# The last phase's final sum as an identity product on TensorE, and five of the eight groups of its norm on VectorE

## The reference

```python
x = x + _L1_conv_ref(_ln_c(x), ...)      # gate: (1x1 conv of y) * x3, added to x
t = _to_tokens(x)                        # points as rows, 96 channels
t = t + _L1_ffn_ref(_ln_t(t), L1_ffn_W1, L1_ffn_b1, L1_ffn_W2, L1_ffn_b2)
# _ln_t:  (v - mean) / sqrt(var + 1e-5) over the 96 channels
# _L1_ffn_ref: q_acc(relu(q_acc(q_mul(x) @ W1) + b1)) @ W2 + b2, q_mul = 8-bit floats, q_acc = 16-bit floats
x = _from_tokens(t, x)
```

## Time and profile before

| what | value |
|---|---|
| median of 3 runs | 3906.69 us (3899.2 to 3909.8) |
| profiled execution, its own time | 3896.73 us |
| its span, first to last instruction | 3894.9 us |
| busy over the span | PE 3001.9 us (77%), DVE 3198.1 us (82%), ACT 2883.9 us (74%), POOL 1723.6 us (44%) |
| phase C, from its first transfer's issue | 2730.99 us to the end |
| mean granted TensorE clock | 0.906 of full speed |

### The profile page before, as it was taken

The page is one execution under the profiler, slowest core; times in us unless marked ns, Lnnn a source line. Parts: engine busy times, 40 slices in busy tenths (PEclk is TensorE's granted clock), DMA queues, the critical chain, the costliest instruction groups (busy, mean ns, idle before and its releaser), DMA issues. The chain is left out here.

```text
span 3894.9 us, 67854 instructions
## 1 busy us (share of the span) xinstructions
PE 3001.9 (77%) x21476; PEld 1980.4 (51%) x21476; DVE 3198.1 (82%) x8112; ACT 2883.9 (74%) x6562; POOL 1723.6 (44%) x2404
## 2 busy tenths in 40 slices
PE   6777776777777777777767999998687878778786
PEld 5556565565655656565543444444344444444443
DVE  4888888888888888888875878888689888898987
ACT  2577777777777777777775555555599999999998
POOL 3777777777777777777650000000121222212121
PEclk8798888888888888888878999999799999999999
DMA  2232333323323232332126777776866666666662
GB/s 58 58 83 66 82 89 76 83 66 82 81 76 90 66 82 69 86 85 73 50 66 163 194 196 196 199 196 177 212 176 177 184 187 181 177 177 189 187 176 68
DMA packets 721626, 484.61 MB, mean 124 GB/s; under 512 B 420796, under 2 KB 700668, under 8 KB 708988
## 3 DMA queue, kind: packets, MB, share of 16 engines
q1 hardware_dynamic: 721276, 480.28, 46.8%
HBM read 278.37 MB, written 201.33 MB: 123 GB/s over the span
## 5 line engine op out<-in xcount | busy, mean ns | idle before, releaser
L1777 POOL TENSOR_SCALAR C_var<-C_st 128x16 f32<-128x16 f32 x64 | 16.6, 259 | 1538.3 <-DVE C_st L175 1538.3
L1404 DVE SCALAR_TENSOR_TENSOR B_y<-B_mid,B_coef,B_y 128x512 f32<-128x512 f32 x768 | 521.3, 747 | 139.5 <-ACT B_y L1371 139.5
L1324 PE MATMUL B_ps_row<-B_z,B_g 128*128 128x512 f32 x1152 | 520.0, 601 | 0.0
L375 DVE TENSOR_SCALAR A_hq<-A_h,A_b 128x512 f16<-128x512 f16 x768 | 294.4, 419 | 234.8 <-ACT A_h L367 228.7
L367 ACT ACTIVATE A_h<-A_hid 128x512 f16<-128x512 f32 x768 | 427.1, 591 | 64.2 <-PE A_hid L354 61.3
L175 DVE BATCH_NORM_STATS2 A_st<-A_xT 128x6 f32<-128x192 f32 x1536 | 443.9, 349 | 27.6 <-ACT A_xT L831 13.6
L367 ACT ACTIVATE C_h<-C_hid 128x512 f16<-128x512 f32 x768 | 426.1, 592 | 15.6 <-PE C_hid L354 8.1
L1444 ACT ACTIVATE C_q<-C_xT,C_shift,C_rstd 128x96 fp8e5<-128x96 f32 x1024 | 391.4, 456 | 45.8 <-POOL C_shift L1784 45.8
L861 ACT ACTIVATE A_xc<-A_xT,A_shift,A_rstd 128x96 f32<-128x96 f32 x1024 | 379.1, 456 | 0.0
L164 POOL TENSOR_TENSOR A_rstd<-A_var,A_expo 128x16 f32<-128x16 f32 x128 | 374.3, 2924 | 10.7
L668 PEld LDWEIGHTS A_fbank<-A_big_w,A_xq 97*128 97x128 f32 x2048 | 322.1, 228 | 29.8 <-issue 11.2
(11 more groups left out here) (160 smaller groups left out, 7314.0 us busy)
## 6 DMA issues: line engine op xcount, KB each, us to landing
A_xq<-in_x SPq DMA_DIRECT2D x32, 1536.0 KB, 8.9
x_scratch<-A_xT SPq DMA_DIRECT2D x64, 768.0 KB, 3.2
x_scratch<-A_x3h SPq DMA_DIRECT2D x64, 768.0 KB, 5.4
B_z<-x_scratch SPq DMA_DIRECT2D x96, 512.0 KB, 5.3
y_scratch<-B_y SPq DMA_DIRECT2D x96, 512.0 KB, 3.6
C_x3q<-x_scratch SPq DMA_DIRECT2D x32, 1536.0 KB, 9.1
C_y3q<-y_scratch SPq DMA_DIRECT2D x32, 1536.0 KB, 15.5
C_xT<-x_scratch SPq DMA_DIRECT2D x64, 768.0 KB, 15.7
```

What stands on the lines that cost most here:

```text
L375: r = dve.tensor_scalar(self.hq[:, b, s], self.h16[:, b, s], self.w["b1"][:, j:j + 1], 0.0, ALU.add, ALU.max)
L1324: m = pe.matmul(bank(c, h), g[c.buf(2)][:, d, :], z[c.buf(NB)][:, half(h), d:d + W], start=(d == 0), stop=(d == 2))
L1404: dve.scalar_tensor_tensor(y, mid[c.buf(2)][:, half(h), t:t + W], coef[c.buf(NB)][:, 3 + t:4 + t], y, ALU.mult, ALU.add).then_inc(ev["sums ...
```

## The change

The final sum of group k (residual plus y16b) is made by PE in PSUM: `result` multiplies y16b (16-bit) by a 96 x 96 identity into the bank and adds the four residual tiles as products with the 128 x 128 identity (before, four transposes into a bank of their own, and the sum on DVE). ACT evicts the bank to `outq` (`out` moves from DVE's list to ACT's). PE makes the sum of group s-2 in slot s behind pe_y (before, the transposes of group s-1 ahead of pe_y), that of group 7 in slot 0 of the next step, so that `steps` gets one step more; ACT evicts group s-3 in slot s, behind the hidden evictions. `dve_y` gets a wait for the sum two groups back. Of the norm's groups, 0, 3 and 6 stay on ACT; 1, 2, 4, 5 and 7 go to DVE as two instructions over the group's four tiles (times the scale, plus the shift), at the end of the slot that `LN_AT` gives; `LN_AT` is unchanged. POOL's waits for the norm follow.

```diff
+ACT_NORMS, DVE_NORMS = (0, 3, 6), (1, 2, 4, 5, 7)
 LN_AT = {6: (1, 0), 7: (1, 1), 8: (1, 2), 0: (0, 3), 2: (0, 4), 3: (0, 5), 4: (0, 6), 5: (0, 7)}
...
+    def norms_done(self, eng, i, k):
+        if k in ACT_NORMS:
+            eng.wait_ge(self.ev["norm2_act"], self.ev.at("norm2_act", i, ACT_NORMS.index(k)))
+        else:
+            eng.wait_ge(self.ev["norm2_dve"], self.ev.at("norm2_dve", i, DVE_NORMS.index(k)))
...
+    def dve_norm(self, dve, i, k):
+        ev, n = self.ev, DVE_NORMS.index(k)
+        t = slice(k * TPC, (k + 1) * TPC)
+
+        dve.wait_ge(ev["ln2"], ev.at("ln2", i, k // 4))
+        if n or begun(i - 1):
+
+            dve.wait_ge(ev["norm2_dve"], ev.at("norm2_dve", i, n) - 1)
+        dve.tensor_tensor(self.xs[:], self.x_of(i)[:, k * CW:(k + 1) * CW].rearrange("p (t c) -> p t c", c=C),
+                          per_token(self.rstd[:, t], TPC), ALU.mult).then_inc(ev["scaled2"], 1)
+        dve.wait_ge(ev["scaled2"], ev.at("scaled2", i, n))
+        dve.tensor_tensor(self.q8[:, t, :], self.xs[:], per_token(self.shift[:, t], TPC), ALU.add,
+                          saturate=False).then_inc(ev["norm2_dve"], 1)
...
-        pe.wait_ge(ev["norm2"], ev.at("norm2", i, k))
+        self.norms_done(pe, i, k)
...
         dve.wait_ge(ev["y16"], ev.at("y16", i, k))
+        if k >= 2:
+
+            dve.wait_ge(ev["c_full"], ev.at("c_full", i, k - 2))
+        elif begun(i - 1):
+            dve.wait_ge(ev["c_full"], ev.at("c_full", i - 1, NK - 2 + k))
...
-                back_uses += [("c", s - 1, 0, "out", s - 1), ("y", s - 1, 0, "y16", s - 1)]
...
+                back_uses.append(("y", s - 1, 0, "y16", s - 1))
+            if s >= 2:
+                back_uses.append(("c", s - 2, 0, "out", s - 2))
+            if s == 0:
+                back_uses.append(("c", NK - 1, -1, "out", NK - 1))
...
-            for n in range(-1, NQ):
+            for n in range(-1, NQ + 1):
...
-            def c_turn(i, k):
+            def result(i, k):
 
                 pe.wait_ge(ev["x1"], ev.at("x1", i, k))
-                bank_free(back, i, "c", k)
+                pe.wait_ge(ev["yb"], ev.at("yb", i, k))
+                bank_free(back, i if k < NK - 1 else i + 1, "c", k)
+                bank = back.bank("c", k)
+                pe.matmul(bank[0:C, 0:CH], id16[:], ff.y16b[:, k % 2, :], start=True, stop=False)
                 for t in range(TPC):
                     n = k * TPC + t
-                    m = pe.transpose(back.bank("c", k)[0:C, t * P:(t + 1) * P], ff.x_of(i)[:, n * C:(n + 1) * C], cst[:])
+                    m = pe.matmul(bank[0:C, t * P:(t + 1) * P], ff.x_of(i)[:, n * C:(n + 1) * C], cst[:],
+                                  start=False, stop=(t == TPC - 1))
                 m.then_inc(ev["c_full"], 1)
...
-                        c_turn(i, s - 1)
                         ff.pe_y(pe, i, s - 1)
+                    if i.real and s >= 2:
+                        result(i, s - 2)
+                    if (i - 1).real and s == 0:
+                        result(i - 1, NK - 1)
...
+                    if (i - 1).real and s < 2:
+                        out(i - 1, NK - 2 + s)
+                    if i.real and s >= 3:
+                        out(i, s - 3)
                     if s in LN_AT:
                         ahead, k = LN_AT[s]
-                        if (i + ahead).real:
+                        if (i + ahead).real and k in ACT_NORMS:
                             ff.act_norm(act, i + ahead, k)
...
-                    if i.real and s >= 1:
-                        out(i, s - 1)
+                    if s in LN_AT:
+                        ahead, k = LN_AT[s]
+                        if (i + ahead).real and k in DVE_NORMS:
+                            ff.dve_norm(dve, i + ahead, k)
```

More of the change, by code:

```diff
@@ L1434, in __init__ @@
         self.shift = sb("shift2", [P, NT], F32)
+        self.xs = sb("xs", [P, TPC, C], F32)
+    def norms_done(self, eng, i, k):
[3 more added lines that the diff above has]
+            eng.wait_ge(self.ev["norm2_dve"], self.ev.at("norm2_dve", i, DVE_NORMS.index(k)))
     def act_norm(self, act, i, k):
         ev = self.ev
-        if k % 4 == 0:
-            act.wait_ge(ev["ln2"], ev.at("ln2", i, k // 4))
-            act.sem_inc(ev.passed, 1)
+        act.wait_ge(ev["ln2"], ev.at("ln2", i, k // 4))
         x = self.x_of(i)
@@ L1445, in act_norm @@
                                scale=self.rstd[:, t:t + 1], bias=self.shift[:, t:t + 1], saturate=False)
-        m.then_inc(ev["norm2"], 1)
+        m.then_inc(ev["norm2_act"], 1)
+    def dve_norm(self, dve, i, k):
[9 more added lines that the diff above has]
+                          saturate=False).then_inc(ev["norm2_dve"], 1)
     def pe_q8(self, pe, step, i, k):
         ev, ring = self.ev, self.ring
-        pe.wait_ge(ev["norm2"], ev.at("norm2", i, k))
+        self.norms_done(pe, i, k)
         name, unit, pos = ring.before(step, "q8", k)
@@ L1512, in phase_c @@
                 front_uses.append(("turn", s - 1, 1, "x1", s - 1))
-                back_uses += [("c", s - 1, 0, "out", s - 1), ("y", s - 1, 0, "y16", s - 1)]
-        ev = Events(nc, ctx, "C_", dict(x1=NK, bn2=NK, ln2=2, ln2_s=6, norm2=NK, q8_full=NK, y_full=NK, c_full=NK, q8c=NK,
+                back_uses.append(("y", s - 1, 0, "y16", s - 1))
[3 more added lines that the diff above has]
+                back_uses.append(("c", NK - 1, -1, "out", NK - 1))
+        ev = Events(nc, ctx, "C_", dict(x1=NK, bn2=NK, ln2=2, ln2_s=6, norm2_act=3, norm2_dve=5, scaled2=5, q8_full=NK, y_full=NK, c_full=NK, q8c=NK,
                                         hidden=NJ * NK, h16=NJ * NK, relu=NK, hq=NK, y16=NK, yb=NK, out=NK, pw_full=NK,
@@ L1524, in phase_c @@
         pw = sb("C_pw", [C, C], F32)
+        id16 = sb("C_id16", [C, C], F16)
         expo = sb("C_expo", [P, NT], F32)
@@ L1612, in _ @@
             pe.wait_ge(setup, 32)
-            pe.wait_ge(setup_dve, 2)
+            pe.wait_ge(setup_dve, 3)
             pe.wait_ge(ffn_cast, 8)
@@ L1673, in _, with out @@
         def _(act):
+            def out(i, k):
+                if k % 4 == 0 and begun(i - 1):
+                    n = f"out_st{k // 4}"
+                    act.wait_ge(ev[n], ev.at(n, i - 1, 0) * 16)
+                act.wait_ge(ev["c_full"], ev.at("c_full", i, k))
+                act.activation(group(outq, k), rows(back.bank("c", k)[0:C, 0:CH]), ACT.Copy).then_inc(ev["out"], 1)
             def body(i):
@@ L1696, in _ @@
             dve.tensor_copy(idb[:], cst[:]).then_inc(setup_dve, 1)
+            dve.tensor_copy(id16[:], cst[0:C, 0:C]).then_inc(setup_dve, 1)
             dve.memset(expo[:], -0.5).then_inc(setup_dve, 1)
@@ L1727, in stats @@
                 m.then_inc(ev["bn2"], 1)
[L1729 to L1738, removed]
             def body(i):
@@ L1759, in _ @@
         def _(pool):
-            pool.wait_ge(setup_dve, 2)
+            pool.wait_ge(setup_dve, 3)
             def norm_terms(q, half):
@@ L1768, in norm_terms @@
                 if begun(q - 1):
-                    pool.wait_ge(ev["norm2"], ev.at("norm2", q - 1, 4 * half + 3))
-                    pool.sem_inc(ev.passed, 1)
+                    for k in ((2, 3), (6, 7))[half]:
+                        ff.norms_done(pool, q - 1, k)
                 earlier = q if half else q - 1
```

## The result

The changed kernel takes **4210.7 us** (median of 4 runs, 4208.8 to 4214.1) against 3903.3 us (4 runs, 3899.2 to 3909.8): ratio 1.0791, 95% interval 1.0776 to 1.0806, so 307 us slower. The forecast was 4210, range 4070 to 4300. The profiled execution took 4211.4 us, its span is 4209.5.

A forecast was written before the change was run, and what follows sets the result against it. The bound was taken to be a slot loop PE, copy, evictions, norm, PE of 4.16 us, not ACT's total. 3896.7 + 252 (31 steps x 8.14) + 56 (clock) + 5 (ends) = 4210 us, range 4070 to 4300.

The forecast's parts named there:

- The loop through DVE: Norms in slots 2, 3 and 5: PE waits for DVE's norm, 6.64 us against 4.16, +7.44 a step; chance 0.84.
- The norm's two instructions: DVE's norm of a group: 0.56 us each plus 0.03 between them, 1.15 us in all.
- Slot 4: Group 6's norm stays on ACT, behind the new eviction: +0.5 us a step, between 0 and 0.7.
- The other slots: Slots 6, 7, 8, 0 and 1 together: +0.2 us a step, between -1.5 and +2.
- The sum on PE: Eight f32 instructions for four transposes: about +0.8 us, PE's own slot 3.2 to 4.0, hidden in PE's wait.
- The clock: PE's products at half clock behind the new 2.6 us waits: +56 us in all, between -8 and +119.
- The ends: Last step's three loops some 0.9 us longer each, one product and one eviction behind the last bias: together +5 us.
- Rival 1: In slot 8, POOL's power blocks DVE's norm of group 2: 2.9 us a step, +90, about 4300 us; chance 0.05.
- rival 2: The loop does not close, engine totals set the step at 32 to 33 us: 3820 to 3850 us; chance 0.07.
- Rival 3: ACT's relief is eaten by PE's 4.0 us and its waits, slots about 4.2: 3890 to 3910 us; chance 0.03.

The follow-up runs named there:

- experiment 8: Changed kernel with the norm first in DVE's slot, ahead of the hidden instructions, instead of last: 3926.47 us.
- experiment 1: Changed kernel with the norms of groups 4 to 7 one slot earlier (slots 1 to 4): 3890.28 us.
- experiment 6: Changed kernel with ten useless products at the end of PE's slots 2, 3 and 5, filling the long waits: 4144.84 us.
- experiment 9: Experiment 1 with the residual brought in by four f32 transposes: 3892.17 us; on top of that, group 5's norm back on ACT: 3887.93 us.
- The sum alone: Changed kernel with all eight norms on ACT, keeping the sum on PE: 3958.47 us, ratio 1.0152.
- experiment 4: Kernel before with the five norms on DVE ahead of its output sum, sum left on DVE, transposes on PE: 4391.8 us.

## Why the prediction was right

**The loop through DVE** was the step that carried the sum, and it is shown, not only argued: laid out as 5.35 + 1.15 + 0.14 = 6.64, it measured 5.35 + 1.13 + 0.14 = 6.62; experiment 8 opens it by order alone and experiment 1 by a slot. PE's turn waits on DVE's second norm instruction 96 times (forecast 93, without the last step), 78 of them for 2.59 or 2.60 (forecast 2.6) and the others for less.

**The norm's two instructions** were 0.54 and 0.56 where 0.56 each was taken, over all 158 records of each line in the window from 2760 to 4180 us.

```profile
L1463 DVE TENSOR_TENSOR C_xs<-C_xT,C_rstd x158: 531/536/545, 2778.9 to 4177.2; 128x384 f32<-128x384 f32 x158
```

```profile
L1466 DVE TENSOR_TENSOR C_q<-C_xs,C_shift x158: 557/559/560, 2779.5 to 4177.8; 128x384 fp8e5<-128x384 f32 x158
```

**Slot 4**, +0.5: 4.64 against 4.16, the wait on ACT 0.61. **The other slots**, +0.2: here two misses cancel, and that is luck. Without falls, in experiment 6, slot 2 lasts 7.43 against 4.53 before, +2.90 and not +2.48: the loop was read off slot 3, but slot 2 begins with a turn that waits for no norm. Slots 6, 7, 8, 0 and 1 together take 17.28 against 17.58, -0.30 and not +0.2. So slots 6 to 2 come to 24.71, forecast 17.84 + 0.2 + 6.64 = 24.68, and the whole step to 42.60, forecast 34.57 + 8.14 = 42.71.

**The sum on PE** is eight records in place of four, as forecast. From the first of these to the turn of the next slot, where PE does not wait, it is 0.88 (3217.01 to 3217.89 in experiment 1), and it hides in PE's wait: experiment 9 takes half of it away for no gain even where PE is busiest.

**The clock**, +56: the step's mean of 44.69 is 2.09 above 42.60, times 31 is 65; the kernel before had 34.86 - 34.58 = 0.28, 9 in all; so +56, and experiment 6 gives 66 against the 65. Here a middle was taken between two bounds, and that it came so near is luck: no row of before told how many waits would be followed by a fall. Counted along PE's timeline, 34 of 77 waits over 2 us (from 2800 us on) have a pair over 1.3 us behind them.

**The ends**, +5: the two spans differ by 314.6. Of this 6.7 lie ahead of PE's first turn of phase C (2777.56 against 2770.84; 2769.8 to 2782.8 in the other traces), where the change touches nothing; 31 x 8.02 = 249 and 56 leave 3. That the total came within 1 us of the forecast is luck, then; that the loop makes most of it is not.

**Rival 1**, DVE blocked by POOL's power: in slot 8 the norm of group 2 does come close to it, as that rival had it.

```profile
3272.99 0.53 DVE L1463 TENSOR_TENSOR C_xs<-C_xT,C_rstd 128x384 f32<-128x384 f32 x1
3273.56 0.56 DVE L1466 TENSOR_TENSOR C_q<-C_xs,C_shift 128x384 fp8e5<-128x384 f32 x1
```

```profile
3273.74 0.45 POOL L1821 TENSOR_SCALAR C_less<-C_st 128x16 f32<-128x16 f32 x1
3274.37 3.04 POOL L1824 TENSOR_TENSOR C_rstd<-C_var,C_expo 128x16 f32<-128x16 f32 x1 [0.18 <-POOL C_less L1821]
```

But the norm is over before the power begins, so phase C does not put the rival to the test. Phase A of the same trace does: there 61 of DVE's sums with both inputs in SBUF lie wholly inside a power, and each takes 0.56, the median of the earlier trace rows. One of them:

```profile
1097.37 0.56 DVE L250 TENSOR_TENSOR A_xT<-A_xT,A_y16b 128x384 f32<-128x384 f32 x1
```

```profile
1096.37 2.90 POOL L164 TENSOR_TENSOR A_rstd<-A_var,A_expo 128x16 f32<-128x16 f32 x1
```

The Trainium skill, "SBUF — State Buffer", section "Who interferes with whom", has the two exclude one another for the whole instruction; the rows of the power do not agree. The prediction leaned on the longest sum, 1.068. None of the long ones lies beside a power, but they are no accident: each of the 30 sums that lie beside POOL's product of 128x384 (L226) took 1.06 to 1.07, half a microsecond more than the rest. One of them:

```profile
1101.10 1.07 DVE L250 TENSOR_TENSOR A_xT<-A_xT,A_y16b 128x384 f32<-128x384 f32 x1
```

```profile
1100.82 2.04 POOL L226 TENSOR_TENSOR A_q<-A_xc,A_rstd 128x384 fp8e5<-128x384 f32 x2
```

These rows do agree with that section of the Trainium skill. So the prediction was right to leave the wait out, but its evidence spoke of another POOL instruction: phase C has the power and not the product, and no norm of DVE took over 0.56 there.

**Rivals 2 and 3**, faster (3820 to 3850) or no change (3890 to 3910) with the loop open: their condition is what experiment 1 makes, and the time was 3890. The point from which rival 2 decides was right, its price was not: the totals do not set the step of 34.7. Rival 3 has the time, but not by its reason, PE's 4.0 a slot: experiment 9 takes load from PE and the step stays.

**Of the expectations behind the prediction that missed, two missed by far.** The sum alone was +58, not +110 to +130: an eviction of 0.48 was charged to every slot, where three of them had a wait to take it. And the norm alone was forecast with the same waits as in both parts, though PE's own slot is shorter there and so each idle piece longer.

## What to carry to other kernels

Where each engine runs a written list, price a moved operation by where it stands in its new list: what is ahead of it there, and what that waits for, becomes part of the next engine's wait. If that loop closes within one slot, put the producer first in its slot, or a slot ahead, before moving any load. A total that falls on the busiest engine need not shorten the step: here three versions with PE at 839 or 759 us of 900 had the same step to 0.02 us.

## What the runs showed of the hardware

Idle time on PE had a second price. Behind waits over 2 us for the norm, the next pair of products ran slow 34 times of 77 in the changed kernel (waits 2.6 at most) and 84 of 90 in experiment 4 (up to 3.5); behind waits of 0.8 to 1.0 in experiment 6, never in 92 (all from 2800 us on). The fall to the lower level (1.2 GHz: granted clock 0.50 over a pair of 1.91, 1.00 over one of 1.02) made useless products pay for themselves: 66 us in the changed kernel, 193 in experiment 4. That experiment 4 falls so often because PE's slot is shorter there (four transposes in place of the sum) agrees with the lengths of the waits, but only filling them was tried.

DVE and POOL hold one another up only with some instructions. DVE's sum gave way to POOL's product of 128x384 (1.06 instead of 0.56), not to its power. POOL gave way to DVE's norm: its short instruction at 3273.74 took 0.45 and ended 0.07 after the norm's second instruction; so did all 31 of its 64 records that lie beside that instruction (0.44 to 0.51), and the other 33 took 0.21. It is off the path here.
